# Low halves of x for the masked layers: from one engine to two, chunk by chunk

## The chip, the cores and the metric

One core of a Trainium2 chip runs the whole program in one launch. The metric is the device time of that launch in microseconds (us): the median of the runs of a kernel. Engines are named as the profile names them: PE (TensorE; PEld are its weight loads), DVE (VectorE), ACT (ScalarE), POOL (GpSimd), and the queue SP, which issues most DMAs.

## The reference

Four layers of cross-attention follow each other, for 4 batches of 1024 tokens of width 512, with one context of 64 keys of width 1024. Layers 0 and 2 ("grouped") normalize x, use 16 heads of 32 over 4 key-value heads, and add the result to x. Layers 1 and 3 ("masked") use 16 heads of 64 and add a bias to two or four of the key columns before the softmax:

```python
# grouped (L0, L2)
xn = rmsnorm(x, norm_w)
q, k, v = xn @ wq, cond @ wk, cond @ wv
attn = softmax(einsum('btgrd,bsgd->bgrts', qg, k) / sqrt(32))
x = x + (attn @ v) @ wo
# masked (L1, L3)
q, k, v = x @ Wq, ctx @ Wk, ctx @ Wv
logits = einsum('bhqd,bhkd->bhqk', q, k) / 8 + col_bias
x = softmax(logits) @ v @ Wo + bo + x
```

## The kernel before

Each matrix product of float32 values is made of three products on PE (`three`, L349 to L353): every operand is held as a high half (a copy by ACT, rounded to the type that PE reads) and a low half (the value less its high half, a subtraction). The function multiplies high by high, high by low and low by high.

The program first projects the context to keys and values. Then comes a loop of eight iterations, one for each pair of layers and each batch. An iteration has four phases, `ph` 0 to 3. Phases 0 and 1 make the scores of the grouped layer for the two blocks of 512 tokens; phases 2 and 3 make those of the masked layer. While phase `ph` makes its scores, it also finishes the block of the phase before: it transposes the probabilities, multiplies by the values and the output weights, and adds the result to x.

The change is at the two places in an iteration where a phase with grouped output ends: the end of phase 1 and the end of phase 2. This text calls them the first and the second boundary. What happens there, engine by engine:

- DVE adds the finished output in bank `OB[c]` to x, chunk by chunk (`xnew`, L863, four chunks `c` of 128x512). These adds write `X[ph - 1]`.
- ACT copies each chunk to `xhl[:, 0, c]`, the high half (L716, semaphore `xb_hi`).
- POOL subtracts: `xhl[:, 1, c]` is `X` less the high half (L1072, semaphore `xb_lo`). Both inputs lie in SBUF. At the second boundary POOL has two more normalizations (L1013) and two scalings of the next weights (L932) ahead of it in its order.
- PE folds weights for the masked layer, eight small groups `t` of matmuls into the four banks `PB` (`fold_bound`, L453 in phase 2, L456 in phase 3). ACT makes their high halves (L677), DVE their low halves (L771, tiles `foldM` and `foldN`; `lo_part` is the helper at L770). Group `t + 4` of PE goes to the bank of group `t`, so it waits for `fold_lo` of group `t` (L443).
- PE then makes the first scores of the phase (tile `SB` from `foldM` and `xhl`). They wait for the fold's low halves of group 6, and chunk by chunk for `xb_hi` and `xb_lo` (L564, L565).

The order on each engine is the order of the code; nothing is scheduled at run time but by semaphores. A line can stand for several tiles: L771 is every low half that DVE makes, so the tile's name tells them apart.

Of the kernel before, what the change touches and what calls it, by code (L numbers as in the profile page):

```python
# [10 lines left out]
ALU = mybir.AluOpType  # L11
# [7 lines left out]
DC = D // P  # L19
# [23 lines left out]
def bass_cross_attention_stack(nc, xT, ctxT, wkvM, wkvG, wqG, woG, wqM, woM, normw, bo, masks, idx, xs):  # L43
# [12 lines left out]
    with ctx:  # L56
        def sb(name, shape, dt=F32):
            return ctx.enter_context(nc.sbuf_tensor(name, shape, dt))

        def sem(name):  # L60
            return ctx.enter_context(nc.semaphore(name))
# [12 lines left out]
        X = [sb(f"x{b}", [P, DC, BLK]) for b in range(NBLK)]  # L74
        xhl = sb("xhl", [P, 2, DC, BLK], F32R)
# [27 lines left out]
        def bank(name):  # L103
# [8 lines left out]
        names = ("ctx_in cx_hi cx_lo w_hi w_lo made taken g_hi ld_w ws_scaled ws_hi ws_lo c_in c_norm "  # L112
                 "c_made c_f c_eq c_m1 c_m2 c_m3 c_both c_sel c_scale bias_a bias_b aux_st zero idented ld_vg "
                 "ld_kg ld_x0 ld_x1 ld_aux ld_kv stored0 stored1 scores copied biased maxed evac "
                 "exped hsummed summed normed trans prodd pt_hi pt_lo mixed ot_hi ot_lo outd xnew xb_hi xb_lo "
                 "qchunk qd q_hi q_lo x_hi x_lo x_sq rmsd sq_added powd invd fold fold_hi fold_lo").split()
        S = {n: sem("s_" + n) for n in names}
        w_in = [sem(f"s_w_in{i}") for i in range(4)]
# [228 lines left out]
        def _(pe):  # L347
# [189 lines left out]
            def scores(it, ph, u):  # L537
                k = 4 * it + ph
                hf, tt = u // 4, u % 4
                if u >= 2 and ph < 2:  # L540
                    pe.wait_ge(S["copied"], 16 * it + 8 * ph + u - 1)
                elif u >= 2:
                    pe.wait_ge(S["biased"], 16 * it + 8 * (ph - 2) + u - 1)
                out = SB[u % 2]
                tok = slice(tt * P, (tt + 1) * P)
                if ph < 2:
                    a = 2 * it + ph
                    if u == 0:
                        pe.wait_ge(S["q_lo"], 4 * a + 3)
                        pe.wait_ge(S["ld_kg"], 64 * (it + 1))  # L550
                    if u == 1:
                        pe.wait_ge(S["q_lo"], 4 * a + 4)
                    for i in range(2):
                        j = 2 * hf + i
                        last = three(out[:, i * 256:(i + 1) * 256], qT[:, 0, j, tok], qT[:, 1, j, tok],
                                     kG[:, 0, j * 256:(j + 1) * 256], kG[:, 1, j * 256:(j + 1) * 256], True, True)
                else:
                    if u == 0:
                        pe.wait_ge(S["fold_lo"], 16 * it + 8 * (ph - 2) + 7)
                    if u == 1:  # L560
                        pe.wait_ge(S["fold_lo"], 16 * it + 8 * (ph - 2) + 8)
                    for c in range(DC):
                        if u == 0:
                            pe.wait_ge(S["xb_hi"], 4 * (2 * it + ph - 2) + c + 1)  # L564
                            pe.wait_ge(S["xb_lo"], 4 * (2 * it + ph - 2) + c + 1)  # L565
                        last = three(out[:, :], xhl[:, 0, c, tok], xhl[:, 1, c, tok],
                                     foldM[:, 0, c, hf * HALF:(hf + 1) * HALF], foldM[:, 1, c, hf * HALF:(hf + 1) * HALF],
                                     c == 0, c == DC - 1)
                last.then_inc(S["scores"], 1)
# [199 lines left out]
        def _(dve):  # L769
# [85 lines left out]
            def xnew(it, ph, c):  # L855

                k = 4 * it + ph
                blk = (ph - 1) % 2
                dve.wait_ge(S["outd"], 4 * (k - 1) + c + 1)
                if ph in (1, 2):  # L860
                    if c == 0:
                        dve.wait_ge(S[f"ld_x{blk}"], 16 * (it + 1))
                    dve.tensor_tensor(X[blk][:, c, :], OB[c][:, :], X[blk][:, c, :], ALU.add).then_inc(S["xnew"], 1)  # L863
                else:
                    dve.scalar_tensor_tensor(out=X[blk][:, c, :], in0=OB[c][:, :], scalar=bout[:, c:c + 1],
                                             in1=X[blk][:, c, :], op0=ALU.add, op1=ALU.add).then_inc(S["xnew"], 1)

            def body(it, first):
                for ph in range(4):
                    k = 4 * it + ph  # L870
                    if ph < 2:
                        a = 2 * it + ph
                        for j in range(4):
                            dve.wait_ge(S["q_hi"], 4 * a + j + 1)
                            lo_part(qT[:, 1, j, :], PB[j][:, :], qT[:, 0, j, :]).then_inc(S["q_lo"], 1)
                            if j == 1:

                                dve.wait_ge(S["qchunk"], 4 * a + 4)
                                dve.tensor_scalar(inv[ph], OB[3][:, 0:TT], 1.0 / D, EPS, ALU.mult, ALU.add
                                                  ).then_inc(S["rmsd"], 1)  # L880
                    else:
                        for t in range(KC):
                            dve.wait_ge(S["fold_hi"], 16 * it + 8 * (ph - 2) + t + 1)
                            (src, hi), (_, lo) = fold_part(ph, t, 0), fold_part(ph, t, 1)
                            lo_part(lo, src, hi).then_inc(S["fold_lo"], 1)
                    out_of = not (first and ph == 0)
                    grouped = ph in (1, 2)
                    for u in range(STEPS):
                        if out_of:
                            pt_lo(it, ph, u)  # L890
                        if grouped and u >= 2 and u % 2 == 0:
                            ot_lo(2 * it + ph - 1, u // 2 - 1)
                        if grouped and u == STEPS - 1:
                            ot_lo(2 * it + ph - 1, 3)
                        evac(it, ph, u, first)
                        if u > 0:
                            sums(k, ph, u - 1, first)
                        if not out_of:
                            m_taken(EARLY + u)
                            if EARLY + u + 4 < MASKED:  # L900
                                w_lo(EARLY + u + 4)
                    sums(k, ph, STEPS - 1, first)
                    if out_of:
                        for c in range(DC):
                            xnew(it, ph, c)

            body(0, True)
            with dve.Fori(1, ITS) as it:
# [10 lines left out]
        def _(pool):  # L919
# [114 lines left out]
            def body(it, first, nxt):  # L1034
                for ph in range(4):
# [31 lines left out]
                            if ph == 3 and u >= 2 and nxt is not None:  # L1067
                                ws_lo(it + 1, u - 2)
                    if ph in (1, 2):
                        for c in range(DC):  # L1070
                            pool.wait_ge(S["xb_hi"], 4 * (2 * it + ph - 1) + c + 1)
                            pool.tensor_tensor(xhl[:, 1, c, :], X[ph - 1][:, c, :], xhl[:, 0, c, :].bitcast(F32),  # L1072
                                               ALU.subtract).then_inc(S["xb_lo"], 1)

            body(0, True, 0)
            with pool.Fori(1, BATCH - 1) as it:
# [49 lines left out]
```

## Time and profile before

| what | value |
|---|---|
| median of 3 runs | 1689.45 us (1689.1 to 1689.66) |
| profiled execution: its own time | 1690.16 us |
| its span | 1688.0 us |
| PE busy | 1617.7 us, 96% of the span |
| DVE busy | 1038.8 us, 62% |
| POOL busy | 782.1 us, 46% |
| ACT busy | 684.9 us, 41% |
| L1072 on POOL (low halves of x) | 64 instructions, 79.5 us |

The span is the time in the profile from the first to the last instruction, and the profiled execution's own time is 2.16 us longer. PE is busy nearly all the time, so a wait of PE is what a change can add or take away. The page's chain of work that ended last is 82% PE, 8% DVE, 4% ACT and 2% POOL.

### The profile page before, as it was taken

To read this page: it belongs to the slowest core of one execution; us is meant where nothing else is said; L and a number is where in the kernel's file an instruction comes from. 1 tells how busy PE (TensorE), PEld (TensorE's weight loads), DVE (VectorE), ACT (ScalarE), POOL (GpSimd) and SP (SyncE) were. 2 spreads that over 40 slices of the span, in tenths; PEclk is the share of its full clock that TensorE was granted. 3 is DMA by queue.
4 is the path that set the end of the run, shared out by engine and by line. 5 is a ranking of instruction groups with operands and counts; after the bars stand their busy time and mean duration, and the time that the engine had idled before them with its cause. 6 is when DMAs were issued, how large, how long until landed. Compare 5 with 4: busy or idle time off the path is not lost.

```text
span 1688.0 us, 25162 instructions
## 1 busy us (share of the span) xinstructions
PE 1617.7 (96%) x8416; PEld 1339.1 (79%) x8416; DVE 1038.8 (62%) x1758; ACT 684.9 (41%) x1193; POOL 782.1 (46%) x745
## 2 busy tenths in 40 slices
PE   8989999999999999999999999999999999999997
PEld 8988778877787878878788777878788787887786
DVE  5545666467655675567654776557664676557763
ACT  3445433453335532453334623354324533345321
POOL 2747334572356542573356623574345723565310
PEclk9999999999999999999999999999999999999999
DMA  7942221222222310322212312322212222222001
GB/s 276 321 137 79 82 63 38 82 77 75 63 93 71 107 39 24 108 82 82 63 52 78 111 31 63 108 81 82 63 38 80 72 82 63 81 77 88 25 1 50
DMA packets 91906, 138.64 MB, mean 82 GB/s; under 512 B 50560, under 2 KB 55168, under 8 KB 85504
## 3 DMA queue, kind: packets, MB, share of 16 engines
q1 hardware_dynamic: 89312, 119.60, 22.6%
q10 hardware_dynamic: 2304, 16.78, 2.4%
q8 instruction: 82, 1.34, 0.3%
q14 instruction: 48, 0.39, 0.1%
q0 software_dynamic: 160, 0.53, 0.1%
HBM read 114.33 MB, written 22.55 MB: 81 GB/s over the span
## 4 chain that ended last, share of the span: by engine, by line
PE 82%; DVE 8%; ACT 4%; issue 3%; POOL 2%; DMA 1%; DVEq 0%; ACTq 0%; POOLq 0%; SPq 0%
PE OB L351 11%; PE OB L353 11%; PE OB L352 11%; PE SB L351 10%; PE SB L353 9%; PE SB L352 9%; PE TB L480 4%; PE MX L351 3%; PE MX L353 2%; PE MX L352 2%; DVE pT L771 2%; PE MX L480 1%; DVE x L863 1%; DVE foldM L771 1%; POOL xqhl L1021 1%
## 5 line engine op out<-in xcount | busy, mean ns | idle before, releaser
L1013 POOL TENSOR_TENSOR prob<-prob,small 128x512 f32<-128x512 f32 x256 | 266.9, 1044 | 586.1 <-DVE small L853 586.1
L727 ACT ACTIVATE prob<-prob 128x512 f32<-128x512 f32 x128 | 81.0, 632 | 507.3 <-DVE prob L841 507.3
L1007 POOL TENSOR_TENSOR prob<-prob,small 128x512 f32<-128x512 f32 x128 | 133.6, 1044 | 168.9 <-DVE small L829 168.1
L351 PE MATMUL OB<-pT,foldN 128*128 128x512 f32 x512 | 205.7, 402 | 6.3 <-DVE pT L771 6.3
L351 PE MATMUL SB<-foldM,xhl 128*128 128x512 f32 x512 | 201.2, 393 | 0.3
L353 PE MATMUL OB<-pT,foldN 128*128 128x512 f32 x512 | 200.4, 391 | 0.0
L352 PE MATMUL OB<-pT,foldN 128*128 128x512 f32 x512 | 200.2, 391 | 0.0
L353 PE MATMUL SB<-foldM,xhl 128*128 128x512 f32 x512 | 199.7, 390 | 0.0
L352 PE MATMUL SB<-foldM,xhl 128*128 128x512 f32 x512 | 199.2, 389 | 0.0
L829 DVE TENSOR_REDUCE small<-prob 128x8 f32<-128x512 f32 x128 | 87.7, 685 | 143.3 <-ACT prob L697 143.2
L835 DVE SCALAR_TENSOR_TENSOR prob<-SB,aux 128x512 f32<-128x512 f32 x128 | 88.2, 689 | 142.1 <-PE SB L353 142.1
L771 DVE TENSOR_TENSOR pT<-TB,pT 128x512 fp32r<-128x512 f32 x192 | 130.4, 679 | 56.3 <-ACT pT L745 54.9
L697 ACT ACTIVATE prob<-SB 128x512 f32<-128x512 f32 x128 | 76.5, 598 | 165.7 <-PE SB L353 164.8
L480 PE MATMUL TB<-ident,prob 128*128 128x128 f32 x768 | 117.9, 276 | 12.3 <-DVE pT L771 11.4
L745 ACT ACTIVATE pT<-TB 128x512 fp32r<-128x512 f32 x192 | 112.8, 588 | 24.7 <-PE TB L480 20.6
L480 PEld LDWEIGHTS TB<-ident,prob 128*128 128x128 f32 x768 | 90.1, 142 | 35.7 <-DVE pT L771 19.5
L351 PEld LDWEIGHTS OB<-pT,foldN 128*128 128x128 f32 x512 | 96.7, 189 | 25.4 <-DVE pT L771 4.9
L353 PEld LDWEIGHTS OB<-pT,foldN 128*128 128x128 f32 x512 | 96.4, 188 | 21.1
L351 PEld LDWEIGHTS SB<-foldM,xhl 128*128 128x128 f32 x512 | 96.1, 188 | 20.9 <-DVE foldM L771 1.3
L353 PEld LDWEIGHTS SB<-foldM,xhl 128*128 128x128 f32 x512 | 96.1, 188 | 20.5
L352 PEld LDWEIGHTS SB<-foldM,xhl 128*128 128x128 f32 x512 | 96.2, 188 | 19.8
L352 PEld LDWEIGHTS OB<-pT,foldN 128*128 128x128 f32 x512 | 96.9, 189 | 17.5
(139 smaller groups left out, 3853.6 us busy)
## 6 DMA issues: line engine op xcount, KB each, us to landing
prob<-in_wkvM_dram SPq DMA_DIRECT2D x32, 512.0 KB, 5.9
ring<-in_wqM_dram SPq DMA_DIRECT2D x64, 256.0 KB, 2.8
ring<-in_woM_dram SPq DMA_DIRECT2D x64, 256.0 KB, 3.4
out_dram<-x ACTq DMA_DIRECT2D x16, 1024.0 KB, 3.9
wraw<-in_wqG_dram SPq DMA_DIRECT2D x8, 1024.0 KB, 7.5
ring<-in_xT_dram SPq DMA_DIRECT2D x32, 256.0 KB, 4.3
wraw<-in_woG_dram SPq DMA_DIRECT2D x8, 1024.0 KB, 5.1
x<-in_xT_dram SPq DMA_DIRECT2D x8, 1024.0 KB, 5.1
```

Source lines behind the costliest of these rows:

```text
L351: pe.matmul(out, a_hi, b_hi, start=start, stop=False)
L352: pe.matmul(out, a_hi, b_lo, start=False, stop=False)
L353: return pe.matmul(out, a_lo, b_hi, start=False, stop=stop)
L480: last = pe.transpose(out[:, tt * P:(tt + 1) * P], pr[:, tt, t * P:(t + 1) * P], ident[:, :])
L697: act.activation(prob[ph][:, u % 4, (u // 4) * HALF:(u // 4 + 1) * HALF], SB[u % 2][:, :], ACT.Copy).then_inc(S["copied"], 1)
L727: act.activation(own, own, ACT.Exp).then_inc(S["exped"], 1)
L745: act.activation(pT[:, t % 2, 0, :], t_bank(ph, t)[:, :], ACT.Copy).then_inc(S["pt_hi"], 1)
L771: return dve.tensor_tensor(out, psum, hi.bitcast(F32), ALU.subtract)
L829: dve.reduce_max(hmax[u % 2], own, AX_X).then_inc(S["maxed"], 1)
L835: dve.scalar_tensor_tensor(out=own, in0=bank, scalar=M_SCALE, in1=row, op0=ALU.mult, op1=ALU.add).then_inc(S["biased"], 1)
L1007: pool.tensor_tensor(own, own, hmax[u % 2].unsqueeze(2).broadcast_to([P, HH, KEYS]), ALU.subtract).then_inc(S["evac"], 1)
L1013: pool.tensor_tensor(own, own, rsum[u % 2].unsqueeze(2).broadcast_to([P, HH, KEYS]), ALU.mult).then_inc(S["normed"], 1)
```

## The change

POOL makes the low halves of chunks 0 and 2 alone. DVE makes those of chunks 1 and 3, right after its four adds to x and ahead of its low halves of the fold. Each engine has a semaphore of its own, and PE waits for the one that belongs to the chunk.

```diff
@@ names
-                 "exped hsummed summed normed trans prodd pt_hi pt_lo mixed ot_hi ot_lo outd xnew xb_hi xb_lo "
+                 "exped hsummed summed normed trans prodd pt_hi pt_lo mixed ot_hi ot_lo outd xnew xb_hi xb_lo_p xb_lo_d "
@@ scores, on PE
                         if u == 0:
                             pe.wait_ge(S["xb_hi"], 4 * (2 * it + ph - 2) + c + 1)
-                            pe.wait_ge(S["xb_lo"], 4 * (2 * it + ph - 2) + c + 1)
+                            pe.wait_ge(S["xb_lo_d" if c % 2 else "xb_lo_p"], 2 * (2 * it + ph - 2) + c // 2 + 1)
@@ body, on DVE
                     if out_of:
                         for c in range(DC):
                             xnew(it, ph, c)
+                    if grouped:
+                        for c in (1, 3):
+                            dve.wait_ge(S["xb_hi"], 4 * (2 * it + ph - 1) + c + 1)
+                            lo_part(xhl[:, 1, c, :], X[ph - 1][:, c, :], xhl[:, 0, c, :]).then_inc(S["xb_lo_d"], 1)
@@ body, on POOL
                     if ph in (1, 2):
-                        for c in range(DC):
+                        for c in (0, 2):
                             pool.wait_ge(S["xb_hi"], 4 * (2 * it + ph - 1) + c + 1)
                             pool.tensor_tensor(xhl[:, 1, c, :], X[ph - 1][:, c, :], xhl[:, 0, c, :].bitcast(F32),
-                                               ALU.subtract).then_inc(S["xb_lo"], 1)
+                                               ALU.subtract).then_inc(S["xb_lo_p"], 1)
```

DVE's order at the first boundary of the loop, before and after in one piece (x is written by the last add, xhl is the half of x, foldM the folded weights):

```order
 L859 REGISTER_ALU
 L863 TENSOR_TENSOR x<-OB,x 128x512
+L771 TENSOR_TENSOR xhl<-x,xhl 128x512 x2
 L771 TENSOR_TENSOR foldM<-TB,foldM 128x4x128
 L771 TENSOR_TENSOR foldM<-MX,foldM 128x4x128
```

Two subtractions now stand between the adds to x and the first low half of the fold; the second boundary reads the same with `foldN`.

POOL's order at the second boundary of the first iteration, before (prob is normalized, wraw is scaled for the next grouped layer):

```order
L1013 TENSOR_TENSOR prob<-prob,small 128x512
L932 TENSOR_TENSOR wraw<-wraw,norms 128x512
L1013 TENSOR_TENSOR prob<-prob,small 128x512
L932 TENSOR_TENSOR wraw<-wraw,norms 128x512
L1072 TENSOR_TENSOR xhl<-x,xhl 128x512 x4
L1013 TENSOR_TENSOR prob<-prob,small 128x512 x3
```

and the same place after (lines below the new ones on DVE have moved by four):

```order
L1017 TENSOR_TENSOR prob<-prob,small 128x512
L936 TENSOR_TENSOR wraw<-wraw,norms 128x512
L1017 TENSOR_TENSOR prob<-prob,small 128x512
L936 TENSOR_TENSOR wraw<-wraw,norms 128x512
L1076 TENSOR_TENSOR xhl<-x,xhl 128x512 x2
L1017 TENSOR_TENSOR prob<-prob,small 128x512 x3
```

Two of four instructions are gone from POOL, and nothing else of it has moved.

## Rows read from the trace of the kernel before

**Rows 1.** The page, part 1: busy time, share of the span, instructions.

```profile
PE 1617.7 (96%) x8416; PEld 1339.1 (79%) x8416; DVE 1038.8 (62%) x1758; ACT 684.9 (41%) x1193; POOL 782.1 (46%) x745
```

**Rows 2.** Waits of PE: who waited for whom, us in total, times, longest.

```profile
PE TB L456 <- DVE foldN L771: 13.1, 8, 1.6
PE TB L453 <- DVE foldM L771: 8.1, 8, 1.0
PE SB L351 <- DVE foldM L771: 3.9, 9, 0.9
```

**Rows 3.** Timeline, first boundary of iteration 4: start, length, instruction, [idle before <- releaser].

```profile
960.35 2.48 DVE L863 TENSOR_TENSOR x<-OB,x 128x512 f32<-128x512 f32 x4
...
961.08 2.42 ACT L716 ACTIVATE xhl<-x 128x512 fp32r<-128x512 f32 x4 [1.69 <-DVE x L863]
...
961.79 4.98 POOL L1072 TENSOR_TENSOR xhl<-x,xhl 128x512 fp32r<-128x512 f32 x4 [0.32 <-ACT xhl L716]
...
964.02 0.69 DVE L771 TENSOR_TENSOR foldM<-TB,foldM 128x512 fp32r<-128x512 f32 x1 [1.18 <-ACT foldM L677]
...
964.86 1.13 PE L453 MATMUL TB<-kv,ring 128*128 128x128 f32 x8 [1.03 <-DVE foldM L771]
...
969.19 0.50 PE L351 MATMUL SB<-foldM,xhl 128*128 128x512 f32 x1
```

**Rows 4.** Timeline, second boundary of the same iteration.

```profile
1012.68 2.48 DVE L863 TENSOR_TENSOR x<-OB,x 128x512 f32<-128x512 f32 x4
...
1014.98 1.04 POOL L932 TENSOR_TENSOR wraw<-wraw,norms 128x512 f32<-128x512 f32 x1
...
1015.98 4.96 POOL L1072 TENSOR_TENSOR xhl<-x,xhl 128x512 fp32r<-128x512 f32 x4
...
1016.34 0.69 DVE L771 TENSOR_TENSOR foldN<-TB,foldN 128x512 fp32r<-128x512 f32 x1 [1.18 <-ACT foldN L677]
...
1017.18 1.10 PE L456 MATMUL TB<-ring,kv 128*128 128x512 f32 x2 [1.65 <-DVE foldN L771]
...
1021.46 0.19 PEld L351 LDWEIGHTS SB<-foldM,xhl 128*128 128x128 f32 x1
```

**Rows 5.** L841 and L1072 alone: duration ns least/median/most.

```profile
L841 DVE TENSOR_TENSOR prob<-prob,small x128: 691/692/1521, 196.5 to 1649.7; 128x512 f32<-128x512 f32 x128
...
L1072 POOL TENSOR_TENSOR xhl<-x,xhl x64: 1257/1277/1292, 183.1 to 1600.8; 128x512 fp32r<-128x512 f32 x64
```

**Rows 6.** Timeline of DVE and POOL at two places where both work.

```profile
118.75 1.04 POOL L1013 TENSOR_TENSOR prob<-prob,small 128x512 f32<-128x512 f32 x1
119.45 1.43 DVE L771 TENSOR_TENSOR foldN<-prob,foldN 128x1024 fp32r<-128x1024 f32 x1 [0.65 <-ACT foldN L623]
...
1065.20 2.55 POOL L1021 TENSOR_TENSOR xqhl<-ring,xqhl 128x512 fp32r<-128x512 f32 x2
...
1066.78 1.52 DVE L841 TENSOR_TENSOR prob<-prob,small 128x512 f32<-128x512 f32 x1
1067.71 1.74 POOL L1029 TENSOR_TENSOR sqsum<-xsq 128x512 f32<-128x512 f32 x1
```

**Rows 7.** Timeline, second boundary of the last iteration, POOL and DVE.

```profile
1597.09 4.97 POOL L1072 TENSOR_TENSOR xhl<-x,xhl 128x512 fp32r<-128x512 f32 x4
...
1599.32 0.69 DVE L771 TENSOR_TENSOR foldN<-TB,foldN 128x512 fp32r<-128x512 f32 x1 [1.18 <-ACT foldN L677]
```

**Rows 8.** Timeline of PE, first boundaries of iterations 0 and 2: waits for a DMA.

```profile
190.69 1.16 PE L453 MATMUL SB<-kv,ring 128*128 128x128 f32 x8 [1.57 <-DMA ring<-in_wqM_dram]
...
579.07 1.16 PE L453 MATMUL SB<-kv,ring 128*128 128x128 f32 x8 [0.47 <-DMA ring<-in_wqM_dram]
```

**Rows 9.** A long wait of PE; a stretch: busy by engine, granted clock, DMA share, GB/s.

```profile
96.41 0.47 PE L351 MATMUL TB<-xqhl,wqo 128*128 128x512 f32 x1 [3.68 <-POOL xqhl L1021]
...
97.00:101.00 4.00, 4.00 (x12) 3.13 (x11) 0.00 (x0) 0.00 (x0) 1.75 (x2) 0.57 0.04 14
```

**Rows 10.** L565 alone: PE's wait instructions at the first scores, ns.

```profile
L565 PEldq EVENT_SEMAPHORE  x64: 51/51/51, 190.8 to 1604.6; - x64
```

## The prediction

> **What bounds the kernel now.** I read the busy shares first. PE is busy 96% of the span, POOL 46%, DVE 62% [rows 1], so work taken from POOL is worth only what PE waited for it. The waits of PE come next. At the two boundaries that the change touches, PE waits for DVE's low halves of the fold, eight times at each, 8.1 and 13.1 us in all, and its first scores wait another 3.9 us for the same DVE tiles [rows 2]. No wait of PE for POOL's halves of x is in that list. The timelines show why. At the first boundary POOL's four subtractions end at 961.79 + 4.98 = 966.77, 2.4 us before the first score matmul at 969.19 [rows 3]. At the second they end at 1015.98 + 4.96 = 1020.94, 0.5 us before the first weight load of the scores at 1021.46 [rows 4]. What does bind is the chain on DVE: first low half of the fold, then group 4 of PE 0.84 us after its start (964.02 to 964.86, 1016.34 to 1017.18) [rows 3, 4], then groups 5 to 7, their halves, and the scores. A delay of that first low half goes straight into PE.
>
> **What is removed.** POOL loses 2 of 4 subtractions at each of 16 boundaries, 1.28 us each [rows 5]. They end before the scores and cover nothing, so I count 0 for them.
>
> **What is added.** DVE gets 32 subtractions of 128x512 with both inputs in SBUF. The trace has that shape as L841, 0.69 us alone [rows 5]; the four adds of x take 2.48 us, which makes 0.61 us from start to start [rows 3]. They go into the idle time of 1.18 us that DVE had ahead of the first low half [rows 3, 4]. Its adds end at 962.83; chunk 3's high half is there at 961.08 + 2.42 = 963.50. Without any quarrel with POOL, chunk 1 runs from 962.8, chunk 3 from 963.50, and the fold's first low half starts at 964.11 where it started at 964.02: 0.09 us late, 16 times, 1.4 us. That is the lower bound.
>
> **DVE and POOL exclude each other here.** L841 has a median of 692 ns and a maximum of 1521 [rows 5]. Where it takes 1.52, it was ready at 1066.78 while the second of two L1021 on POOL ran until 1067.75; it ended at 1068.30, that is 0.55 us after POOL. POOL's next instruction L1029, shown from 1067.71 for 1.74, ended at 1069.45, 1.15 us after DVE [rows 6]. L771 with both inputs in SBUF does the same: ready at 119.45, POOL's L1013 until 119.79, end at 120.88, 1.09 us later for twice the elements [rows 6]. So each waits for the other's running instruction to end, and DVE needs 0.55 us from there. The adds to x and the fold's low halves have one input in PSUM and take their usual time beside L1072 [rows 3]. The Trainium skill (SBUF — State Buffer, Who interferes with whom) has this as a rule against the change: a VectorE instruction with two SBUF inputs contends with a GpSimd instruction that reads SBUF, and whichever issued first holds the other off entirely. By that rule the new DVE work cannot run beside the POOL work that it is meant to relieve; the trace agrees with its 1521 ns.
>
> First boundary, times of [rows 3]. POOL's chunk 0 ends at 961.79 + 1.28 = 963.07. DVE's chunk 1 has waited since 962.83 and ends at 963.62. POOL's chunk 2 has waited since 963.03 or so; with 1.2 us after DVE (between the 1.15 of [rows 6] and the 1.28 alone of [rows 5]) it ends at 964.82. DVE's chunk 3 ends at 965.37. The fold's first low half starts 0.08 us before that end (0.69 less 0.61), at 965.29: 1.27 us late.
>
> Second boundary, [rows 4]. POOL is behind: L932 runs until 1016.02. DVE's chunk 1, ready at 1015.16, ends at 1016.57; POOL's chunk 0 at 1017.77; DVE's chunk 3 at 1018.32; the first low half starts at 1018.24 instead of 1016.34: 1.90 us late. In the last iteration there are no L932: chunk 0 of POOL ends at 1597.09 + 1.28 = 1598.37, then 1598.92, 1600.12, 1600.67, start at 1600.59 instead of 1599.32 [rows 7]: 1.27 us.
>
> In iteration 0 PE later waits 1.57 us for a weight DMA at the first boundary, in iteration 2 0.47 us [rows 8]; those take back 1.27 and 0.47. The transfers were issued as banks and ring slots came free of groups 0 to 3, which do not move. Everything after group 4 (high halves on ACT, low halves on DVE, transposes, scores) hangs on PE and moves with it. PE waits for a second POOL or DVE semaphore in one more instruction of 51 ns and one register operation per boundary [rows 10]; they stand behind six matmuls in the queue, which hide them, so 0, and 1.6 us if all 32 were exposed.
>
> Sum: first boundaries 8 x 1.27 - 1.27 - 0.47 = 8.4; second 7 x 1.90 + 1.27 = 14.6; together 23.0 us. The profiled execution took 1690.16 us, which becomes 1713.2; the median of the runs lies 0.71 below, so 1712.4.
>
> **The rivals.**
>
> *DVE keeps the port.* The sum rests on POOL's chunk 2, already waiting, getting its turn between DVE's two. Rows 6 show only one direction: DVE, waiting, got in between two POOL instructions that followed each other at once. They have no case of two such DVE instructions back to back with POOL waiting. If DVE's second follows at once, 0.61 us later, the first low half starts at 963.62 + 0.61 - 0.08 = 964.15 (0.13 late), at the second boundary at 1017.10 (0.76), in the last iteration 0.13. That is 6 x 0.13 + 7 x 0.76 + 0.13 = 6.2 us: 1695.7. Against it: one that waits has been served before one that only follows in the case that we have. The skill (SBUF — State Buffer, A bandwidth-pool intuition that's wrong) measured a GpSimd transfer as blocked until VectorE's end and about 115 ns more, a gap in which a ready VectorE instruction could slip. In [rows 6] no such gap is seen: POOL ended 1.15 us after DVE where its kind takes 1.28.
>
> *PE's clock falls too.* After a wait of 3.68 us the granted clock was 0.57 on average from 97 to 101, which loses 4 x 0.43 = 1.7 us; the longest wait at the boundaries now is 1.65 and there it does not fall [rows 2, 9]. The second boundaries would wait 1.65 + 1.90 = 3.55 us, seven times, close to the one that fell. If half fell: 1712.4 + 6 = 1718; all: 1724.3. Part would hide, since the first microseconds after such a wait are fold groups with DVE and ACT between them.
>
> *No price for the collision:* the 1.4 us above, 1690.9. Against it stand both cases of [rows 6].
>
> *Faster.* POOL's recorded ends are rough. If its fourth chunk really landed 0.5 us after 1020.94, the scores would be held by POOL, and halving its work would give PE back at most the 3.9 us before first scores [rows 2]: 1685.5. It decides only if DVE's additions stay within its idle 1.18 us, so without the collision too; and at the first boundary POOL has 2.4 us in hand.
>
> **Chances.** Forecast 0.55 (own range 1708 to 1717); DVE keeps the port 0.25; clock falls 0.11; no price 0.05; faster 0.04. A change of 0.2% is 3.4 us, about what a measurement of this kernel can tell from none. Slower by more: the first three, 0.91; within: 0.06; faster: 0.03, a part of the last case being too small to see. The range reaches down to take in the port case and up into the clock case: 1693 to 1719.
>
> **What would show it.** On DVE, between the adds and the first `foldM` or `foldN` low half: two `xhl` rows, of which the second, and at the second boundary both, read clearly over 0.69 us (about 0.8, 1.7 at the first; 1.4, 1.7 at the second). On POOL: the second `xhl` of a boundary stretched at the first, the first at the second. PE's waits on `foldM` near 8 x 2.3 and on `foldN` near 8 x 3.5 us. The clock at 1.00 from 1012 to 1022. Wrong: if DVE's second `xhl` follows the first at once, the port rival holds; if PE waits for `xhl` of POOL, the chain was misread.

## The result, and the profile after

The changed kernel takes 1732.29 us (median of 4 runs, 1726.98 to 1736.98); the kernel before took 1689.28 in 4 runs beside them. The ratio is 1.0255, 95% interval 1.0237 to 1.0273. The profiled execution took 1730.33 us by its own time, with a span of 1728.5: 40.5 us more than the span before. The forecast of 1712.4 had the sign and half of the size. The four runs of the changed kernel have mean granted clocks of 0.987, 0.987, 0.983 and 0.980 with 1726.98, 1730.33, 1734.25 and 1736.98 us, so how often the clock falls differs from one execution to the next, and every count of falls below is that of one profiled execution.

The page after, part 1, in the form of [rows 1]:

```profile
PE 1634.8 (95%) x8416; PEld 1347.3 (78%) x8416; DVE 1081.0 (63%) x1790; ACT 684.8 (40%) x1193; POOL 753.6 (44%) x713
```

PE has as many instructions as before and is busy 17.1 us longer with them. No wait explains that: the same matmuls ran slower for a part of the time. DVE's 32 new instructions raised its busy time by 42.2 us, 1.32 us each.

Who PE waited for, after (total us, times, longest), against [rows 2]:

```profile
PE TB L456 <- DVE foldN L771: 27.0, 8, 3.5
PE TB L453 <- DVE foldM L771: 17.5, 8, 2.2
...
PE TB L351 <- POOL xqhl L1025: 6.8, 9, 3.7
...
PE SB L351 <- DVE foldM L771: 4.9, 15, 0.8
```

The two waits of the boundaries grew from 13.1 to 27.0 and from 8.1 to 17.5 us, together 23.3. The first scores add 1.0, and the wait for POOL at the start of an iteration is what it was (6.8 in place of 6.7). The two waits for a weight DMA at first boundaries [rows 8], 2.0 us, are gone.

The tile `xhl` after: its subtractions on POOL and on DVE, duration in ns least/median/most, to set against [rows 5]:

```profile
L1076 POOL TENSOR_TENSOR xhl<-x,xhl x32: 1275/1713/1721, 183.4 to 1635.9; 128x512 fp32r<-128x512 f32 x32
L771 DVE TENSOR_TENSOR xhl<-x,xhl x32: 856/1668/1752, 184.4 to 1636.5; 128x512 fp32r<-128x512 f32 x32
```

None of DVE's 32 took the 0.69 us of the shape alone; the shortest took 0.86. Half of POOL's or more took at least 0.4 us more than before.

DVE at both boundaries of iteration 4, after, against [rows 3, 4]:

```profile
979.01 2.48 DVE L863 TENSOR_TENSOR x<-OB,x 128x512 f32<-128x512 f32 x4
981.42 2.53 DVE L771 TENSOR_TENSOR xhl<-x,xhl 128x512 fp32r<-128x512 f32 x2
983.87 0.68 DVE L771 TENSOR_TENSOR foldM<-TB,foldM 128x512 fp32r<-128x512 f32 x1
...
1032.62 2.48 DVE L863 TENSOR_TENSOR x<-OB,x 128x512 f32<-128x512 f32 x4
1035.02 3.17 DVE L771 TENSOR_TENSOR xhl<-x,xhl 128x512 fp32r<-128x512 f32 x2
1038.11 0.68 DVE L771 TENSOR_TENSOR foldN<-TB,foldN 128x512 fp32r<-128x512 f32 x1
```

The rows behind the dots are the second boundary. The first low half of the fold starts 983.87 - 979.01 = 4.86 us after the adds, where it was 3.67: 1.19 late. At the second it is 1038.11 - 1032.62 = 5.49 instead of 3.66: 1.83 late.

PE after its waits, in the changed kernel: second boundary of iteration 2 (first row), of iteration 4, and first boundary of iteration 5:

```profile
641.02 1.10 PE L456 MATMUL TB<-ring,kv 128*128 128x512 f32 x2 [3.46 <-DVE foldN L771]
...
1038.94 2.05 PE L456 MATMUL TB<-ring,kv 128*128 128x512 f32 x2 [3.46 <-DVE foldN L771]
1040.78 1.78 PE L456 MATMUL MX<-ring,kv 128*128 128x512 f32 x2
...
1184.33 1.13 PE L453 MATMUL TB<-kv,ring 128*128 128x128 f32 x8 [2.21 <-DVE foldM L771]
1185.30 1.58 PE L453 MATMUL MX<-kv,ring 128*128 128x128 f32 x8
```

The same two matmuls of group 4 take 1.10 us after a wait of 3.46 in iteration 2, and 2.05 after the same wait in iteration 4. In the last pair of rows the wait was only 2.21 and the next group takes 1.58 instead of 1.06. Four stretches follow; each row has its length, the busy time and instruction count of PE, PEld, DVE, ACT and POOL, then the granted clock, the DMA share and GB/s:

```profile
636.00:640.00 4.00, 1.56 (x4) 0.38 (x2) 4.00 (x4) 3.80 (x8) 4.00 (x5) 1.00 0.88 260
640.00:644.00 4.00, 2.98 (x7) 1.43 (x8) 3.71 (x7) 1.32 (x3) 1.40 (x1) 1.00 0.37 98
...
1039.00:1042.00 3.00, 3.00 (x4) 1.42 (x5) 1.93 (x4) 0.60 (x1) 0.31 (x1) 0.50 0.10 23
...
1184.00:1188.00 4.00, 3.67 (x23) 3.70 (x24) 3.12 (x6) 1.19 (x2) 0.00 (x0) 0.71 0.67 227
```

The granted clock is 0.50, that is 1.2 GHz instead of 2.4, from 1039 to 1042; it stays at 1.00 in iteration 2. I added up the lost clock over the whole span, stretch by stretch of 2 us, as (1 - granted clock) times the stretch. Before it is 4.7 us, at the start (96) and the end (1656, 1686). After it is 23.3. (Each sum has about 1 us behind the last instruction.) Each fall costs 1.7 us, as in [rows 9], and some come doubled at 3.4:

| place | clock falls, after | lost |
|---|---|---|
| second boundaries (wait 3.46 us, the last 2.82) | 7 of 8: at 242, 440, 836, 1038, 1240, 1438, 1638, two of them doubled | 15.3 us |
| first boundaries (wait 2.2 us) | 2 of 8: at 188 and 1184 | 3.4 us |
| elsewhere, as before | 96, 1696, 1728 | 4.5 us |

The budget closes: 23.3 us of waits for group 4, 1.0 of first scores, 2.0 less of waits for a DMA, and 18.6 of clock make 40.9, against 40.5 of span. The place agrees too. From the first fold matmul of a boundary to the first masked score PE took 150.7 us at the 16 boundaries together before, and 190.0 after: 39.3 of the 40.5 us.

### The profile page after: what moved, and what is told of

It reads as the page before. It is cut to its first block, busy times and chain, and to the rows that moved or that the text cites. A ratio compares the mean times of both kernels' runs of the same rounds, so it can differ in the third digit from the quotient of the medians.

```text
span 1728.5 us, 25176 instructions
## 1 busy us (share of the span) xinstructions
PE 1634.8 (95%) x8416; PEld 1347.3 (78%) x8416; DVE 1081.0 (63%) x1790; ACT 684.8 (40%) x1193; POOL 753.6 (44%) x713
## 4 chain that ended last, share of the span: by engine, by line
PE 79%; DVE 11%; issue 3%; ACT 3%; POOL 2%; DMA 1%; DVEq 0%; SPq 0%; ACTq 0%; POOLq 0%
PE OB L351 10%; PE OB L353 10%; PE OB L352 10%; PE SB L351 9%; PE SB L353 9%; PE SB L352 9%; PE TB L480 4%; PE MX L351 3%; DVE xhl L771 3%; PE MX L353 2%; PE MX L352 2%; DVE x L863 2%; DVE pT L771 2%; PE MX L480 1%; DVE foldM L771 1%
## 5 line engine op out<-in xcount | busy, mean ns | idle before, releaser
L351 PE MATMUL OB<-pT,foldN 128*128 128x512 f32 x512 | 205.8, 402 | 6.3 <-DVE pT L771 6.3
L351 PE MATMUL SB<-foldM,xhl 128*128 128x512 f32 x512 | 201.2, 393 | 1.0 <-DVE foldM L771 1.0
L352 PE MATMUL OB<-pT,foldN 128*128 128x512 f32 x512 | 200.2, 391 | 0.0
L352 PE MATMUL SB<-foldM,xhl 128*128 128x512 f32 x512 | 199.3, 389 | 0.0
L480 PE MATMUL TB<-ident,prob 128*128 128x128 f32 x768 | 117.9, 276 | 12.2 <-DVE pT L771 11.3
L745 ACT ACTIVATE pT<-TB 128x512 fp32r<-128x512 f32 x192 | 112.8, 588 | 24.7 <-PE TB L480 20.6
L351 PEld LDWEIGHTS OB<-pT,foldN 128*128 128x128 f32 x512 | 96.7, 189 | 25.3 <-DVE pT L771 4.9
L351 PEld LDWEIGHTS SB<-foldM,xhl 128*128 128x128 f32 x512 | 96.1, 188 | 22.2 <-issue 2.4
L352 PEld LDWEIGHTS SB<-foldM,xhl 128*128 128x128 f32 x512 | 96.2, 188 | 19.8
L352 PEld LDWEIGHTS OB<-pT,foldN 128*128 128x128 f32 x512 | 96.9, 189 | 17.5
```

Source lines behind the costliest of these rows:

```text
L351: pe.matmul(out, a_hi, b_hi, start=start, stop=False)
L352: pe.matmul(out, a_hi, b_lo, start=False, stop=False)
L480: last = pe.transpose(out[:, tt * P:(tt + 1) * P], pr[:, tt, t * P:(t + 1) * P], ident[:, :])
L745: act.activation(pT[:, t % 2, 0, :], t_bank(ph, t)[:, :], ACT.Copy).then_inc(S["pt_hi"], 1)
```

## The experiments

The theory they tested: the two DVE subtractions collide with POOL's at the SBUF port, DVE's fold halves come 1.2 and 1.8 us late, and PE's longer waits then let its clock fall. Rivals: the collision costs by another way than through the fold's first low half; the clock falls for another reason; POOL's relief or DVE's busy time counts by itself. In the diffs, - is the changed kernel and + the experiment, unless it says otherwise. Ratios are to runs of the kernel before that were taken beside the experiment. "Clock lost" is the sum explained above (4.7 before, 23.3 after).

**POOL's halves left out.** POOL makes no low half of x, so chunks 0 and 2 keep old ones, and PE does not wait for them. DVE's order is that of the change.

```diff
-                    if ph in (1, 2):
-                        for c in (0, 2):
-                            pool.wait_ge(S["xb_hi"], 4 * (2 * it + ph - 1) + c + 1)
-                            pool.tensor_tensor(xhl[:, 1, c, :], ...)
```

> The changed kernel without POOL's subtractions of chunks 0 and 2, so those low halves are not computed; DVE keeps its two. Theory (DVE and POOL exclude each other): at the first boundary POOL is idle, DVE's two xhl take 0.7 us each and the fold starts 0.1 us late; at the second only L932's counterpart is still in the way, 0.76 us. PE waits 8 x 1.1 and 8 x 2.4 us, time 1695 to 1705 with a few falls of the clock. Rival (two more DVE instructions on the chain are dear by themselves): 1712 us or more, with PE waits as in the changed kernel.

Measured: 1697.16 us (1696.09 to 1698.68), 1.0043 [1.0026, 1.006]. Span 1696.3, clock lost 11.3. Waits of PE, and the subtractions on DVE:

```profile
PE TB L456 <- DVE foldN L772: 18.4, 8, 2.4
...
PE TB L453 <- DVE foldM L772: 9.0, 8, 1.2
```

```profile
L772 DVE TENSOR_TENSOR xhl<-x,xhl x32: 677/687/1499, 183.1 to 1606.5; 128x512 fp32r<-128x512 f32 x32
```

With POOL out of the way DVE's median is 687 ns again, and the first boundary costs 0.9 us in all. At the second, the tail of POOL's scaling of weights (L936 in the changed kernel) still meets DVE's first (1499 at most), the wait is 2.4 us, and the clock fell at 3 of 8. So 35 of the 43 us hang on POOL and DVE working at once, not on the 32 instructions. This also shows that the falls come without the full collision.

**No collision, same lateness.** POOL makes all four halves as before. In the place of DVE's two subtractions stand reductions of a constant tile, which have one input: four at the first boundary and five at the second, to be as late as the collision made it. Their results are not used.

```diff
-                        for c in (1, 3):
-                            dve.wait_ge(S["xb_hi"], 4 * (2 * it + ph - 1) + c + 1)
-                            lo_part(xhl[:, 1, c, :], X[ph - 1][:, c, :], xhl[:, 0, c, :]).then_inc(S["xb_lo_d"], 1)
+                        for n in range(4 if ph == 1 else 5):
+                            dve.reduce_max(spare[:, 8 * n:8 * n + 8],
+                                           still[:, :].rearrange("p (h k) -> p h k", k=KEYS), AX_X)...
```

> The kernel before (POOL makes all four chunks) with 4 reductions of 128x512 on DVE at the first boundary and 5 at the second, ahead of the fold; a reduction has one SBUF input, starts every 0.61 us, and its result is not used. Theory (all the time comes through PE's longer wait for the first low half): the fold starts 1.2 and 1.8 us late as in the changed kernel, PE waits 17.5 and 27 us, the clock falls as often, 1728 to 1737 us, though no DVE instruction waits for POOL. Rival (the collision itself costs more than the wait it makes): 1712 us or less.

Measured: 1730.4 us (1727.75 to 1733.97), 1.0246 [1.0228, 1.0264]. Waits 16.8 (2.1 at most) and 26.6 (3.3), clock lost 26.9, with a fall at all 8 second boundaries and one of 8 first ones. The reductions take 672 to 677 ns, and POOL's instructions keep their time:

```profile
L1083 POOL TENSOR_TENSOR xhl<-x,xhl x64: 1262/1276/1290, 183.6 to 1633.9; 128x512 fp32r<-128x512 f32 x64
```

The whole loss is there with no collision at all. So it comes through the lateness of the fold's first low half; what else the collision does (POOL's stretched instructions, say) costs nothing that this pair could tell, within some 3 us, the width of either interval.

**The same instruction count, one input.** As above with two reductions at each boundary.

```diff
+                        for n in range(2 if ph == 1 else 2):
+                            dve.reduce_max(spare[:, 8 * n:8 * n + 8],
+                                           still[:, :].rearrange("p (h k) -> p h k", k=KEYS), AX_X)...
```

> As the run with 4 and 5 reductions, with 2 and 2: the same number of DVE instructions as the change adds, without a second SBUF input. Theory: they fit into DVE's idle 1.18 us, fold starts at most 0.1 us late, 1689 to 1692 us, clock as before. Rival (any work added there costs its length): 1709 us.

Measured: 1690.22 us (1687.42 to 1690.63), 1.0 [0.999, 1.001]; waits 8.1 and 13.1 as before. Two instructions of 674 ns at 16 places, in DVE's idle time, cost nothing.

**The same, two inputs.** The two reductions become two subtractions of the constant tile from itself, into `xsq`, whose values from there nobody reads. POOL makes its four halves.

```diff
+                        for n in range(2 if ph == 1 else 2):
+                            dve.tensor_tensor(xsq[:, n, :], still[:, :], still[:, :], ALU.subtract)...
```

> The kernel before (POOL makes all four chunks) with 2 subtractions of 128x512 on DVE at each boundary, ahead of the fold, both inputs in SBUF, result not used: as the run with 2 and 2 reductions, which cost nothing, but for the second SBUF input. Theory (only the second SBUF input makes DVE and POOL exclude each other, and they alternate): the two take 0.8 to 1.8 us each, the fold starts 1.2 and 1.9 us late, PE waits 17.5 and 27 us, the clock falls, 1726 to 1737 us. Rival (two more DVE instructions at most): 1690 us.

Measured: 1730.85 us (1728.41 to 1735.55), 1.0251 [1.023, 1.0271]. Waits 17.5 and 27.0, clock lost 27.0 with falls at 7 of 8 second and 2 of 8 first boundaries. DVE's rows of the new subtractions:

```profile
L914 DVE TENSOR_TENSOR xsq<-still x32: 856/1666/1751, 183.4 to 1636.9; 128x512 f32<-128x512 f32 x32
```

These are the changed kernel's numbers to the nanosecond or two. Between the last two experiments the constant tile that is read, the place and the count are the same. The instruction differs: a reduction with one SBUF input that writes 8 columns, or a subtraction with two that writes 512. That is worth 40.6 us. The wider output is not the cause, as DVE's low halves of the fold write 512 columns to SBUF from one SBUF input and one in PSUM, and take 0.69 us beside POOL's L1072 [rows 3]. The Trainium skill (SBUF — State Buffer, Who interferes with whom) says that a VectorE instruction with two SBUF inputs contends with a GpSimd instruction that reads SBUF; this pair agrees, with 674 ns against 1666.

**POOL's relief alone.** POOL makes chunks 0 and 2, and nobody makes 1 and 3 (old ones are used, and PE does not wait for them).

```diff
-                    if grouped:
-                        for c in (1, 3):
-                            dve.wait_ge(S["xb_hi"], 4 * (2 * it + ph - 1) + c + 1)
-                            lo_part(xhl[:, 1, c, :], X[ph - 1][:, c, :], xhl[:, 0, c, :]).then_inc(S["xb_lo_d"], 1)
```

> The kernel before with POOL's chunks 1 and 3 left out and nothing in their place (those low halves are not computed): the half of the change that takes work away. Theory (POOL's four subtractions end before the scores): 1689 to 1690.5 us, no difference. Rival (POOL's last subtraction holds the first scores): 1685 us.

Measured: 1688.01 us (1685.18 to 1690.23), 0.9994 [0.9984, 1.0003], waits of PE 8.0 and 13.1. The half of the work that POOL loses was worth nothing, as counted.

**DVE's two later.** The subtractions of the change move from ahead of the fold's low halves to between them, after groups 3 and 4.

```diff
+                            if t in (3, 4):
+                                c = 2 * t - 5
+                                dve.wait_ge(S["xb_hi"], 4 * (2 * it + ph - 2) + c + 1)
+                                lo_part(xhl[:, 1, c, :], X[ph - 2][:, c, :], xhl[:, 0, c, :]).then_inc(S["xb_lo_d"], 1)
...
-                    if grouped:
-                        for c in (1, 3):
-                            dve.wait_ge(S["xb_hi"], 4 * (2 * it + ph - 1) + c + 1)
-                            lo_part(xhl[:, 1, c, :], X[ph - 1][:, c, :], xhl[:, 0, c, :]).then_inc(S["xb_lo_d"], 1)
```

> The changed kernel with DVE's chunks 1 and 3 behind the fold's low halves 3 and 4 in place of ahead of them all. Theory (the cost is the late first low half): POOL's two chunks run undisturbed, the first low half starts as before the change, PE waits 8 and 13 us, the clock does not fall there; low halves 5 and 6 come about 0.5 us late, 8 us in all: 1690 to 1698 us. Rival (the collision costs wherever it stands): 1720 us or more.

Measured: 1695.5 us (1695.04 to 1696.89), 1.0037 [1.0024, 1.0049]. The tile `xhl` there:

```profile
L1076 POOL TENSOR_TENSOR xhl<-x,xhl x32: 1260/1274/1287, 182.8 to 1603.0; 128x512 fp32r<-128x512 f32 x32
L771 DVE TENSOR_TENSOR xhl<-x,xhl x32: 678/681/683, 187.4 to 1607.6; 128x512 fp32r<-128x512 f32 x32
```

POOL's two are done by then, so nothing collides, and the waits of groups 4 are 8.1 and 13.1 as before. What is left is the wait of the first scores, 7.7 us instead of 3.9, and in the profiled execution a doubled fall of the clock near its end, 1.7 us more than before. Where in DVE's order the same two instructions stand is worth 37 us.

**PE's waits filled.** Three runs put matmuls with a result that nobody reads ahead of PE's wait for group 4. If the clock falls because PE stands still there, filling the wait keeps it up. First at both boundaries (6 and 12 matmuls), then at the second alone with 6, then with 3.

```diff
+                    if t == 4:
+                        pe.wait_ge(S["xnew"], 4 * (k - 2) + 1)
+                        for n in range(6 if ph == 2 else 12):
+                            pe.matmul(OB[0][:, :], wqo[:, 0, 0, 0:P], wqo[:, 0, 0, :], start=True, stop=True)
```

```diff
+                    if t == 4 and ph == 3:
+                        pe.wait_ge(S["xnew"], 4 * (k - 2) + 1)
+                        for n in range(6):
+                            pe.matmul(OB[0][:, :], ident[:, :], aux[:, 0:BLK], start=True, stop=True)
```

The third has `range(3)` in the second form.

> The changed kernel with matmuls of 128x512 on PE between fold groups 3 and 4, into a bank that is overwritten later: 6 at the first boundary, 12 at the second, 1.4 and 2.8 us, which fit into the waits of 2.2 and 3.5 us. Theory (17 of the 40 us are the clock falling after those waits): the granted clock stays at 1.00 at the boundaries, 1710 to 1714 us, that is the 23 us forecast for the collision alone. Rival (the clock is not the cause of the rest): 1728 to 1737 us, unchanged.

> The changed kernel with 6 plain float32 matmuls of 128x512 (0.43 us each, 2.6 us) on PE between fold groups 3 and 4 at the second boundary alone; their result is overwritten. It repeats the filled run with 12 instructions fewer at that place and none at the first, since 36 more instructions per iteration brought six waits of about 3.9 us marked issue at the start of an iteration. Theory (the clock falls because PE waits 3.5 us idle): no fall at second boundaries, first boundaries fall as before in about 2 of 8, 1712 to 1718 us. Rival (the fall has another cause): 1728 us or more, or if the issue waits return, 1740.

> The changed kernel with 3 plain float32 matmuls on PE (1.3 us) in the wait of 3.5 us at the second boundary: 6 instructions more per iteration in place of 12 or 36. Theory: the rest of the wait is 2.2 us, as at the first boundary, where the clock falls in 2 of 8; so 3 or 4 falls fewer, each worth about 1.7 us, 1722 to 1726 us, if PE's instruction loading stays as in the changed kernel (82 packets on the instruction queue). Rival (the added instructions bring the issue waits back): 85 packets or more and 1745 us or more.

Measured, both filled: 1746.22 us (1745.24 to 1747.76), 1.0332 [1.0315, 1.035]. The total missed its expectation by far. Waits of PE, PE itself at the second boundary of iteration 4, the granted clock there and at the start of an iteration, and the queue that brings instructions:

```profile
PE TB L353 <- issue: 22.8, 6, 4.2
...
PE TB L457 <- DVE foldM L775: 6.7, 8, 0.9
...
PE TB L460 <- DVE foldN L775: 4.5, 6, 0.8
```

```profile
493.63 0.41 PE L353 MATMUL TB<-xqhl,wqo 128*128 128x512 f32 x1 [3.93 <-issue]
...
1043.12 3.30 PE L444 MATMUL OB<-wqo 128*128 128x512 f32 x12
1047.17 1.10 PE L460 MATMUL TB<-ring,kv 128*128 128x512 f32 x2 [0.76 <-DVE foldN L775]
```

```profile
494.00:498.00 4.00, 4.00 (x13) 3.10 (x12) 0.00 (x0) 0.29 (x1) 0.00 (x0) 0.59 0.03 6
...
1044.00:1048.00 4.00, 3.24 (x13) 2.16 (x12) 4.00 (x5) 1.93 (x4) 3.56 (x3) 1.00 0.72 200
```

```profile
q8 instruction: 89, 1.46, 0.3%
```

At none of the 16 boundaries did the clock fall, though DVE was as late as in the changed kernel. That part of the theory held. But the clock lost is 22.9 us in all, as a wait came up that neither kernel has: in six of eight iterations PE stands 3.8 us on average near the iteration's start for nothing that the profile names, and then the clock falls there. The instruction queue moved 89 packets, where before and after it moved 82. I take these waits for PE's longer loop being fetched again; that is a guess from the packets and was not taken apart. The step from the second boundary of iteration 0 to the first of iteration 1 has no such wait. From DVE's adds to its next adds it took 142.2 us, where the changed kernel took 144.8 (a fall in it) and the kernel before 141.2. Of those 2.6 us the fall is 1.7; the other 0.9 is that group 4 came 0.9 us less late there.

Second alone with 6: 1757.84 us (1753.98 to 1760.37), 1.0404 [1.0385, 1.0423], slower still. The fillers were mis-sized. A plain float32 matmul is two instructions here, and six of them take twice the 2.6 us that was expected:

```profile
1048.97 5.31 PE L444 MATMUL OB<-aux,ident 128*128 128x512 f32 x12
1054.12 1.02 PE L460 MATMUL TB<-ring,kv 128*128 128x512 f32 x2
```

That is longer than the wait of 3.46. PE's time between groups 3 and 4 is 4.99 us, 1.5 more at each second boundary, some 13 in all, so this run did not leave the lateness as it was. Its "issue" waits moved to another place (15.5 us, 6 times, at L352's scores, and 3.6 at L351, against 3.0 in the changed kernel) with 85 packets. The clock held at the filled second boundaries, but fell at 6 of 8 first ones, after waits of 2.2 us, and at 5 of the 6 long issue waits, so the clock lost is 23.7, as good as unchanged. The longer fillers and the waits for issue (16 us more of them) are about the 28 us by which its span is longer than that of the changed kernel. It had no fall at a second boundary, as the theory had it; the total went the way of the rival on the issue waits, with the fillers' own length beside it.

With 3: 1723.22 us (1723.19 to 1723.25), 1.0199 [1.0182, 1.0216]; 82 packets and 10.3 us of issue waits in short pieces. The three take 2.7 us and not 1.3, and PE waits another 0.90 and not 2.2:

```profile
1032.00 2.74 PE L444 MATMUL OB<-aux,ident 128*128 128x512 f32 x6
...
1035.63 1.10 PE L460 MATMUL TB<-ring,kv 128*128 128x512 f32 x2 [0.90 <-DVE foldN L775]
```

Group 4 is as late as in the changed kernel (3.46 us behind group 3). The second boundaries have no fall, the first two of 8, and the clock lost is 9.7 us instead of 23.3. The time lies in the range that was expected, but by another sum: 13.6 us of clock came back where three or four falls were counted on, and the issue waits took 7 of them. As they grew with the packets at 82, the packets do not explain those. More work for PE made the kernel 9 us faster than the changed one.

**ACT's order, on the kernel before.** This asks what the waits of PE at the boundaries were worth in the first place. DVE's idle 1.18 us ahead of the first low half is a wait for ACT's copy of the folded group, which stands behind four copies of x. Here the two kinds alternate. The diff is to the kernel before.

```diff
+                            if t < DC:
+                                act.wait_ge(S["xnew"], 4 * (k - 2) + t + 1)
+                                act.activation(xhl[:, 0, t, :], X[ph - 2][:, t, :], ACT.Copy).then_inc(S["xb_hi"], 1)
...
-                    if grouped:
-                        for c in range(DC):
-                            act.wait_ge(S["xnew"], 4 * (k - 1) + c + 1)
-                            act.activation(xhl[:, 0, c, :], X[ph - 1][:, c, :], ACT.Copy).then_inc(S["xb_hi"], 1)
```

> The kernel before, POOL with all four chunks; ACT makes the high halves of the fold groups 0 to 3 each ahead of one high half of x, where it made all four of x first. Theory (the boundary is bound by DVE's first low half of the fold, which waits 1.18 us for ACT): that low half starts 1.2 us earlier, PE waits 0 and 0.45 us at the boundaries in place of 1.03 and 1.65, 1670 to 1674 us. Rival (the wait moves to POOL's low halves of x, now 1 us later against earlier scores): 1678 us or more, with waits of PE for POOL xhl.

Measured: 1679.09 us (1678.16 to 1682.36), 0.9945 [0.9929, 0.9962]: 10 us faster than the kernel before, where 15 to 19 were expected. Its waits:

```profile
PE TB L456 <- DVE foldN L770: 1.8, 5, 0.4
...
PE SB L453 <- DMA ring<-in_wqM_dram: 1.6, 3, 0.7
PE TB L456 <- DMA ring<-in_woM_dram: 1.3, 3, 0.6
```

The waits of group 4 for DVE, 21.2 us before, are gone but for 1.8. Some of the weights' transfers are now last, and PE never waits for POOL's halves. From the first fold matmul to the first masked score PE takes 138.3 us in place of 150.7: of 19.4 us of wait taken away, 7 came back inside this stage, as the groups behind group 4 took longer. What holds each of those was not taken apart.

**The same, with the fourth add to x behind the first low half.**

```diff
+                            if t == 0:
+                                xnew(it, ph - 1, 3)
...
-                        for c in range(DC):
+                        for c in range(DC - 1 if grouped else DC):
```

> As the run with ACT's order changed, and DVE makes the fold's first low half ahead of its fourth add to x. Theory: at the second boundary PE's remaining 0.45 us goes too, 3 us less than that run, 1667 to 1671 us. Rival (the later fourth chunk of x delays its low half on POOL and with it the scores): the same or up to 5 us more than that run.

Measured: 1679.61 us (1677.88 to 1681.07), 0.9944 [0.9927, 0.996], the same as without it; 3 us less were expected. The stage from the first fold matmul to the first score takes 140.5 us against 138.3. Group 4's waits for DVE are gone altogether, and the waits for weight transfers grew, the largest to 2.2 us in all. DVE is no longer last there, so making it earlier still brings nothing.

**The better order, with the split.** The alternating order of ACT, POOL's chunks 0 and 2, and DVE's two subtractions after groups 3 and 4. The diff shows what DVE gets beside ACT's new order.

```diff
+                            if t in (3, 4):
+                                c = 2 * t - 5
+                                dve.wait_ge(S["xb_hi"], 4 * (2 * it + ph - 2) + c + 1)
+                                lo_part(xhl[:, 1, c, :], X[ph - 2][:, c, :], xhl[:, 0, c, :]).then_inc(S["xb_lo_d"], 1)
```

> The last one together with ACT's changed order (high halves of the fold and of x in turn), which alone gave 1679 us. Theory (with PE no longer waiting for the first low half, DVE's two extra instructions among the later low halves are on the chain): 1680 to 1688 us, no better than ACT's order with POOL making all four chunks. Rival (POOL's four chunks hold the scores there, so that the split pays now): under 1677 us.

Measured: 1686.78 us (1685.36 to 1690.56), 0.9985 [0.9975, 0.9994], with a new wait for `foldN` at the transposes (3.5 us, 7 times). The ratios 0.9985 and 0.9945 make the split cost some 7 us even in its best place here, so POOL should keep all four.

## Why the prediction was right and wrong

*What bounds the kernel.* Right. In each run without a filler the time moved the way of PE's waits at the boundaries and its clock, and with no busy time of DVE, ACT or POOL. With ACT's order changed only some 12 of 19 us of wait arrived.

*Removed work worth 0.* Right: 1688.01 against 1689.04.

*Added work alone, 0.09 us late 16 times.* Right, as far as it can be seen. The reductions show 0 and, with POOL silent, the first boundaries 9.0 against 8.1 us. The 1.4 us could not be told from nothing.

*The collision.* Right in mechanism and size. Forecast: 1.27 and 1.90 us late; measured 1.19 and 1.83. The two waits were given as 8 x 2.3 and 8 x 3.5 and read 17.5 and 27.0. They grew by 23.3 us where the sum has 24.7 before its DMA terms, 1.27 and 0.47; the DMA waits gave back 2.0. So the net of this term is 21.3 against 23.0. The profile had a case for each direction [rows 6], and these were enough.

*DVE keeps the port.* Refuted. With two subtractions of DVE back to back, POOL's waiting one got in between: the pair takes 2.53 us at the first boundary, where 0.80 + 0.61 = 1.4 would be the time if DVE had kept the port. The chance of 0.25 was too high for what [rows 6] already showed.

*No price* was refuted by the 43 us, *faster* by the run with POOL's relief alone.

*The clock.* This is the step that failed: the sum put the fall of PE's clock at nothing, and it was 18.6 of the 40.5 us. The sum read "everything after group 4 moves with it" at an unchanged rate of PE, and "the clock at 1.00 from 1012 to 1022" was given as a sign; it was 0.50 from 1039 to 1042, the same place in the shifted time. The clock stood among the rivals with a chance of 0.11, priced at 1.7 us a fall over the seven second boundaries of 3.55 us. The price was right. Three things about it were wrong:

1. The chance. [rows 9] had one wait of 3.68 us that ended in a fall, and [rows 2] had 1.65 without one. A forecast wait of 3.55 lay at the upper end of that gap, so the row that it was nearest to spoke for the fall. Behind the first microseconds the same trace has one more wait over 1.65 us, 4.64 us for DVE's `pT` at 1656.49, and the clock fell right after it. In the changed kernel it fell at 6 of the 7 second boundaries that waited 3.46 us, and at the last one, after 2.82. This should have been the forecast, not a rival; all seven falling would have given 1724.3.
2. The first boundaries. They were left out, as their waits of 2.2 us looked short. Two of 8 fell.
3. Doubled falls of 3.4 us, two of them. None stands in the trace of before for a wait. The first two points and this one make up the loss: (7 + 2) x 1.7 for the second boundaries with their doubled ones and 2 x 1.7 for the first are 18.7, against 18.6 measured.

The cover that I named, "part would hide, since the first microseconds are fold groups with DVE and ACT between them", did not hide enough to see: the steps from DVE's adds at a second boundary to those at the next first are 143.6 us without a fall, 145.5 to 146.0 with one, and 147.0 and 147.1 with a doubled one, so the whole 1.7 per fall arrives or nearly so (the steps before the change differ among themselves too, from 141.8 to 142.3 behind iteration 0). Behind iteration 0 the step is 144.8, with one fall, where it was 141.2 before: again 1.9 and 1.7. The range ended at 1719, where a case that the text itself priced at 1724.3 was cut off.

The runs show the chain link by link. The wait made by other means costs the same (1730.4), the collision by other data costs the same (1730.85), and filling the wait takes the falls away at all 16 boundaries. That a fall at a boundary costs its 1.7 us is read from the steps and the lost clock; no run took the falls away and changed nothing else. How often the clock fell, by the length of PE's wait at a boundary:

| kernel, boundary | longest wait | falls |
|---|---|---|
| before, second | 1.65 us | 0 of 8 |
| POOL's halves left out, first | 1.2 | 0 of 8 |
| reductions 4 and 5, first | 2.1 | 1 of 8 |
| changed, first | 2.2 | 2 of 8 |
| two inputs, first | 2.2 | 2 of 8 |
| second boundary filled with 3, first | 2.2 | 2 of 8 |
| second boundary filled with 6, first | 2.2 | 6 of 8 |
| POOL's halves left out, second | 2.4 | 3 of 8 |
| reductions 4 and 5, second | 3.3 | 8 of 8 |
| changed, second | 3.5 | 7 of 8 |
| two inputs, second | 3.5 | 7 of 8 |

What decides in a single case between 2.1 and 2.4 us, or why one wait of 3.46 passed in iteration 2, stays open: the same wait at the same place in the code went either way.

## What to carry to other kernels

Before work moves from POOL to DVE, ask what POOL will be doing at that moment and how many SBUF inputs DVE's instruction has: the same two subtractions cost 43 us beside POOL and 6 us a few instructions later, and two reductions with one input cost nothing even beside POOL. Price a new wait of PE in two ways, once as a wait and once as a fall of its clock, and when the trace has a fall at about the forecast length, put the fall into the sum and not among the rivals. An order on a third engine can be worth more than a share of the work: ACT's two kinds of copy in turn gave 10 us.

## What the hardware did that I had not expected

- PE's clock fell to 1.2 GHz after waits of only 2.2 us, with PE busy before and after, at 1 to 6 of 8 like places. Each fall cost 1.7 us, now and then 3.4.
- POOL and DVE took turns, instruction by instruction, when both had two queued: DVE's median went from 692 to 1668 ns and POOL's from 1277 to 1713.
- Added matmuls in PE's loop, meant to cost nothing, brought waits of up to 4.2 us for "issue", together 22.8 us, with 89 instead of 82 packets of the instruction queue; with three fillers they were 10.3 us at 82 packets. The cause stays open. Three fillers at each second boundary gained 9 us against the changed kernel; 6 and 12 at the two boundaries lost 14.
